# A merged attention, MLP and recurrence kernel: the gate reads the normalised output from PSUM, and TensorE takes two steps of its loop in another order

## The reference, cut to what matters

```python
# layer 0, last part
ln_out = layernorm(x, ln3_s, ln3_b)
x = x + gelu(ln_out @ w1 + b1) @ w2 + b2
# layer 1
xa = ln(x) * ln1_w + ln1_b
sx = previous token's xa - xa
xxx = tanh((xa + sx * maa_x) @ maa_w1)          # the mixer
xk, xw, xv, xr, xg = xa + sx * (maa_stack + xxx @ maa_w2)
w = exp(-exp(time_decay + tanh(xw @ td_w1) @ td_w2))
r, k, v = xr @ Wr.T, xk @ Wk.T, xv @ Wv.T
g = silu(xg @ Wg.T)
# per step and head: out = r . (u * k v + s);  s = k v + w * s
og = (out - mean_head) / sqrt(var_head + 1e-5)   # per head
og = og * gn_w + gn_b                            # the affine copy
x1 = x + (og * g) @ Wo.T                         # gate, output projection
# then the channel mix on x1: two shifts, key, receptance, value
```

## Time and profile before

| | |
|---|---|
| median of three runs | 1197.81 us (1195.29 to 1200.35) |
| span of the profiled execution, first to last instruction | 1193.3 us |
| its mean granted TensorE clock | 0.990 |
| PE busy | 1126.9 us (94%) |
| DVE busy | 968.7 us (81%) |
| ACT busy | 774.8 us (65%) |
| POOL busy | 594.3 us (50%) |
| the chain that ended last | PE 72%, DVE 16%, issue 8%, ACT 2% |

### The profile page before, as it was taken

How to read it: one execution, slowest core, us unless ns; L and a number is a source line. 1 busy time by engine, 2 the same in 40 slices (tenths; PEclk the granted TensorE clock), 3 DMA queues, 4 the chain that set the end, 5 groups by cost and what they waited for, 6 DMA issues and landing times.

```text
span 1193.3 us, 35515 instructions
## 1 busy us (share of the span) xinstructions
PE 1126.9 (94%) x13568; PEld 955.6 (80%) x13568; DVE 968.7 (81%) x1677; ACT 774.8 (65%) x1750; POOL 594.3 (50%) x520
## 2 busy tenths in 40 slices
PE   5899999999999999999999999999999999888898
PEld 5889898889989877777888788877888787667687
DVE  5987778787777761288999999999999999999964
ACT  5778777778778755556755566556755565557475
POOL 5787887877787840243343433434343434343221
PEclk9999999999999989999999999999999999989999
DMA  9400000011111100000000000000000000000001
GB/s 332 139 4 1 0 0 4 20 47 38 46 40 39 45 2 1 1 2 1 1 1 1 2 1 1 0 0 0 0 0 0 0 1 1 10 10 18 18 36 54
DMA packets 25535, 27.31 MB, mean 23 GB/s; under 512 B 2336, under 2 KB 20064, under 8 KB 25056
## 3 DMA queue, kind: packets, MB, share of 16 engines
q1 hardware_dynamic: 25440, 25.99, 6.6%
HBM read 21.79 MB, written 4.19 MB: 22 GB/s over the span
## 4 chain that ended last, share of the span: by engine, by line
PE 72%; DVE 16%; issue 8%; ACT 2%; POOL 1%; DMA 0%; DVEq 0%; ACTq 0%; POOLq 0%
PE psum L953 10%; PE psum L353 9%; PE psum L962 7%; PE psum L267 5%; PE psum L336 5%; PE psum L368 4%; PE psum L1042 4%; PE psum L297 3%; PE psum L1079 3%; DVE shared L1771 3%; PE psum L280 3%; DVE shared L1765 2%; PE psum L1127 2%; PE psum L310 2%; PE psum L1002 2%
## 5 line engine op out<-in xcount | busy, mean ns | idle before, releaser
L1771 DVE TENSOR_TENSOR_SCAN shared<-late_wT,shared 128x512 f32<-128x512 f32 x128 | 184.5, 1442 | 4.4
L863 POOL TENSOR_TENSOR late_xm<-late_mixed,late_xa 128x512 f32<-128x512 f32 x80 | 96.0, 1207 | 162.3 <-DVE late_mixed L1739 156.0
L232 POOL TENSOR_TENSOR shared<-shared,att_row_max 128x512 f32<-128x512 f32 x128 | 132.7, 1056 | 17.4 <-DVE att_row_max L564 17.4
L353 PE MATMUL psum<-shared 128*128 128x128 f32 x1024 | 126.2, 277 | 0.0
L453 ACT ACTIVATE shared<-shared 128x512 f32<-128x512 f32 x128 | 80.4, 631 | 67.9 <-POOL shared L232 67.8
L962 PE MATMUL psum<-w,late_hT 128*128 128x256 f32 x512 | 122.1, 383 | 1.0 <-ACT late_hT L1352 0.9
L872 POOL TENSOR_TENSOR shared<-shared,late_rT 128x512 f32<-128x512 f32 x32 | 41.1, 1284 | 163.6 <-DVE shared L1771 163.6
L353 PEld LDWEIGHTS psum<-shared 128*128 128x128 f32 x1024 | 120.6, 193 | 0.2 <-ACT shared L462 0.2
L564 DVE TENSOR_REDUCE att_row_max<-shared 128x8 f32<-128x512 f32 x128 | 86.9, 680 | 41.0 <-POOL shared L225 41.0
L953 PE MATMUL psum<-late_glnT,w 128*128 128x256 f32 x512 | 118.4, 384 | 1.8 <-ACT late_glnT L1343 1.8
L1765 DVE TENSOR_TENSOR shared<-psum,shared 128x504 f32<-128x504 f32 x128 | 86.7, 678 | 39.1 <-PE psum L1079 37.8
(11 more groups left out here) (170 smaller groups left out, 2656.7 us busy)
## 6 DMA issues: line engine op xcount, KB each, us to landing
shared<-in_enc SPq DMA_DIRECT2D x64, 128.0 KB, 2.6
out<-x SPq DMA_DIRECT2D x16, 256.0 KB, 2.0
x<-in_x SPq DMA_DIRECT2D x7, 512.0 KB, 9.0
w<-in_w SPq DMA_DIRECT2D x2, 1024.0 KB, 16.9
shared<-in_cross_mask SPq DMA_DIRECT2D x1, 1024.0 KB, 11.6
shared<-in_w_qkv SPq DMA_DIRECT2D x1, 768.0 KB, 4.5
x<-in_x SPq DMA_DIRECT2D x2, 256.0 KB, 3.7
shared<-in_w_kv SPq DMA_DIRECT2D x1, 512.0 KB, 12.6
```

Of the source, the lines that this page charges most:

```text
L232: nc.gpsimd.tensor_tensor(zs, zs, peak.unsqueeze(2).to_broadcast([P, PAIRS, S]), ALU.subtract).then_inc(shifted, 1)
L353: last = nc.tensor.matmul(dst[:, half * P:(half + 1) * P], w[:, kb, c0 + half * P:c0 + (half + 1) * P], src[:, u % 2, kb, 0:P], start=(kb ...
L863: nc.gpsimd.tensor_tensor(xm[:, m % 2, :, :].rearrange("p h (b t) -> p (h b) t", t=S), mixed[:, m % 2, :, :].rearrange("p h (b t) -> p (h ...
L1771: nc.vector.tensor_tensor_scan(states, wT[:, u, half, :, :, :].rearrange("p j b t -> p (j b t)"), states, 0.0, ALU.mult, ALU.add).then_inc ...
```

## The change

The affine copy writes its result back into its own PSUM bank (`even`) instead of the SBUF tile `onT`, and the gate reads it there. So the bank is busy for longer, and what next writes it (`bonus_sums`, and in the last run `transpose_on`) waits for `y_ready` instead of `onT_copied`. The copy itself no longer waits for the gate of the run before. On TensorE `bonus_sums(s)` and `project_out(s - 2)` move behind `mlp_transpose(s + 3)` and `mixer(s + 1)`.

```diff
-        onT = core.shared[:, 13328:13840]
@@ bonus_sums
                 if later(r - 1):
-                    pe.wait_ge(onT_copied, r - 1)
+                    pe.wait_ge(y_ready, r - 1)
@@ transpose_on
                 if is_last(r):
-                    pe.wait_ge(onT_copied, r)
+                    pe.wait_ge(y_ready, r)
@@ body of TensorE
                     if n == 1:
+                        if mlp_run:
+                            mlp_transpose(s + 3)
+                        if mixing:
+                            mixer(s + 1)
                         if now:
                             bonus_sums(s)
                         if there(s - 2):
                             project_out(s - 2)
-                        if mlp_run:
-                            mlp_transpose(s + 3)
-                        if mixing:
-                            mixer(s + 1)
@@ copy_on of ScalarE
-                if later(r):
-                    act.wait_ge(y_ready, r)
                 for half in range(HALVES):
-                    last = nc.scalar.activation(onT[...], even[...],
+                    last = nc.scalar.activation(even[...], even[...],
@@ apply_gate of VectorE
-                nc.vector.scalar_tensor_tensor(out=yT[:, :], in0=onT[:, :], scalar=0.5, ...
+                nc.vector.scalar_tensor_tensor(out=yT[:, :], in0=even, scalar=0.5, ...
```

More of the change, by code:

```diff
@@ L1456, in copy_on @@
                 act.wait_ge(onT_ready, r + 1)
-                if later(r):
-                    act.wait_ge(y_ready, r)
                 for half in range(HALVES):
-                    last = nc.scalar.activation(onT[:, half * RT:(half + 1) * RT], even[:, half * RT:(half + 1) * RT],
+                    last = nc.scalar.activation(even[:, half * RT:(half + 1) * RT], even[:, half * RT:(half + 1) * RT],
                                                 ACT.Identity, scale=col(core, "gn_w", half), bias=col(core, "gn_b", half))
@@ L1827, in apply_gate @@
                     dve.wait_ge(out_ready, r)
-                nc.vector.scalar_tensor_tensor(out=yT[:, :], in0=onT[:, :], scalar=0.5, in1=gates[:, u, :], op0=ALU.mult,
+                nc.vector.scalar_tensor_tensor(out=yT[:, :], in0=even, scalar=0.5, in1=gates[:, u, :], op0=ALU.mult,
                                                op1=ALU.mult).then_inc(y_ready, 1)
```

## The result

The changed kernel took 1234.82 us (median of four runs, 1233.11 to 1237.93) against 1198.79 us before: ratio 1.0316, 95% interval 1.029 to 1.0342. It is slower, as forecast, by 36 us where 25.7 were forecast. (The ratio is as recorded; the two medians alone give 1.030, inside the interval.) The median lies at the upper end of the forecast range of 1211 to 1235, and the ratio taken on the 1197.81 us of the forecast gives 1235.7, just beyond it. The span of the profiled execution went from 1193.3 to 1232.3 us, the mean granted clock from 0.990 to 0.985.

A forecast was written before the change was run, and what follows sets the result against it. The prediction took TensorE to bound the loop, 37.57 us of work in a 38.40 us period. Terms 18.7 + 2.15 + 1.6 + 2.3 + 1.0 = 25.7 us on 1197.8 gave 1223.5 us, range 1211 to 1235.

The forecast's parts named there:

- The transposes and the mixer wait for steps that stand behind the gate on DVE: On PE after spread(s, 1): both wait for DVE's residual and mixer input; +1.87 us in each of ten bodies.
- The gate 0.68 us, the fight with POOL handed on to the read, 0.60 us gained: DVE's gate L1828 falls from 1.51 to 0.68 us, POOL's L846 blocks the read L1782; DVE gains 0.60 us per body.
- The copy unchanged: ScalarE's affine copy pair, now writing PSUM, still takes 1.02 us, with 0.3 us either way.
- PE idles 2.2 us ... after another 0.35 us: PE, body 7: 2.2 us idle before the MLP's transposes L938, then 0.35 us more before the mixer.
- From the mixer's start to `spread(s, 2)`: PE, body 7: 2.49 us as after a gap, plus 2.64 us for bonus sums and projection with no wait.
- The clock: Rival: PE's gaps drop the clock to 1.2 GHz in four or more of 13 bodies, 2.3 us each, 1233 to 1253; chance 0.11.
- Body 13, 2.3 us: Body without MLP: 2.64 us put behind the mixer, DVE having perhaps 0.3 us slack; 2.3 us more, bounds 0 and 2.64.
- body 14, 1.0: Body 14 loses between 0 and 1.87 us, 1.0 taken.
- Bodies 0 and 1, 1.6: Bodies without a gate: bonus sums lose the wait that hides them, 0.81 us each, 1.6 us in all.
- Not slower: Rival: transposes and mixer fill the gate's wait and the shorter gate pulls everything forward, 1189 us, or near 1198; chance 0.08.
- half absorbed: Rival: DVE's slack shortens its later steps and PE's waits in bodies 12 to 15, 1204 to 1212 us; chance 0.04.
- gate still held up: Rival: PSUM as input brings nothing, DVE's chain stays, +2.47 us per body instead of 1.87, 1229.5 us; chance 0.05.

The follow-up runs named there:

- the order alone: Kernel before with only TensorE's changed order, the affine copy staying in SBUF: 1261.98 us, ratio 1.0535.
- DVE's order turned round: Changed kernel with mlp_residual and mixer_input put ahead of apply_gate and read in DVE's step 0: 1214.84 us, ratio 1.0137.
- the PSUM half alone: Changed kernel with TensorE's order of before, affine copy and gate still in PSUM: 1199.04 us, ratio 1.0017.
- the sums behind the mixer: Changed kernel with the two sum_heads directly behind mixer(s + 1), bonus sums and projection behind them: 1232.24 us, a single run.
- The filled gap: Changed kernel with the four transposes of spread(s, 1) done five times over in bodies 2 to 13: 1226.95 us, ratio 1.0243.
- the head sums in the gap: Changed kernel with the two sum_heads of run s - 1 moved ahead of mlp_transpose: 1214.70 us, ratio 1.0139.

## Why the prediction was right and wrong, point by point

The direction and the mechanism of the waits were right. Two steps of the sum failed. The larger is the clock: the sum has nothing for it, and it cost 9.2 us of the span. The smaller is the stretch from the mixer's start to `spread(s, 2)`, put at 5.13 us and measured at 5.44, 3.3 us over eleven bodies.

- *The transposes and the mixer wait for steps that stand behind the gate on DVE.* Right, shown by three runs: the order alone loses more, DVE's order turned round gives 1.0 us per period back, and the PSUM half alone does next to nothing.
- *The gate 0.68 us, the fight with POOL handed on to the read, 0.60 us gained.* Right: 0.66, 0.92, 0.61. The Trainium skill, page "SBUF — State Buffer", section "Who interferes with whom", says that a DVE instruction with at most one SBUF input, outside the 2-port modes, does not contend with GpSimd, and that one with two does when GpSimd reads SBUF. The trace agrees: beside POOL's operation the gate takes 0.66 us and the read 0.92.
- *The copy unchanged.* Right: 0.99 against 1.02 us. The page "ScalarE: Activation LUTs", section "Step-by-step: what each stage is for", of the Trainium skill says that ScalarE writes PSUM faster than SBUF. The trace agrees, by 0.03 us for the pair, too little to count.
- *"PE idles 2.2 us ... after another 0.35 us", mixer at 5.88 us after `transpose_on`.* Right: the mixer starts 5.87 us after it, in body 8.
- *"From the mixer's start to `spread(s, 2)`" 2.49 + 2.64 = 5.13.* This step failed by 0.3 us in each body: the measured 5.44. I took mixer and sums as one block of 2.49 us, but the change puts bonus sums and projection between them, and the two no longer overlap: 0.13 us. The bonus sums take 0.92 us to the next start and not 0.81, the projection 1.90 and not 1.83 (840.76, 841.68, 843.58): 0.18 more. With the sums behind the mixer the period is 40.33, which is near my 38.44 + 1.87 in part by luck: the stretch is 5.21 there, not 5.13, and the spread behind it is 0.05 shorter. The step is 3.3 us of the 13.3 by which the span's growth was missed.
- *The clock.* This is the larger error, 9 us. I made it a rival with a chance of 0.11, on the ground that the gap is framed by dense work, and left it out of the sum. The filled gap shows that the ground does not hold. A fall of the clock in the loop was one of my own signs of being wrong. My evidence was misread too: I wrote that longer gaps in the tail had no such sequel, but behind the waits of 2.27 and 1.41 us in body 13 of the kernel before (they end at 1021.59 and 1024.99), this window shows one:

```profile
1027.00:1030.00 3.00, 3.00 (x20) 0.50 0.00 0
```

  The price per fall was wrong as well: 1.3 us in the short ones and 3.2 to 3.3 in the long ones, not 2.3. Four falls came behind the new gaps, in bodies 2, 7, 11 and 13, at 9.2 us together. The rival had put 1233 us on four of them, and the kernel took 1234.8; that these are so near is in part luck, since two falls cost 1.3 us and two 3.2 to 3.3, where four at 2.3 were assumed, and the 3.3 us of the step above are not in the 1233.
- *Body 13, 2.3 us.* Right without the clock fall behind the mixer's wait, as the filled gap shows; *body 14, 1.0*: 0.6. *Bodies 0 and 1, 1.6*: 2.0; what the 0.4 are stays open.
- *Not slower, half absorbed, gate still held up.* None of them: nothing was given back in bodies 2 to 12.

What decides in which bodies the clock falls was not separated from the gap's place in time. That it is not the gap's length alone, the traces show in body -1, where all ten kernels run the same code and the mixer waits some 2.18 us, until between 480.5 and 484.5 us. Within 1.6 us of the wait's end the clock falls in four of them: the PSUM half alone, DVE's steps forward, and the head sums in either place. The window in the kernel before, and the same in the kernel with the PSUM half alone (us, busy and count, granted clock):

```profile
482.00:485.00 3.00, 2.34 (x15) 1.00 0.00 0
```

```profile
482.00:485.00 3.00, 3.00 (x11) 0.50 0.00 0
```

## What to carry to other kernels

A step is moved ahead of a wait only if its own inputs are ready by then: read when the other engine produces them, in that engine's own order. Here 0.8 us of waiting became 2.6 (2.20 from the end of the spread, 0.44 us after its start at 835.71, to 838.35, and 0.36 ahead of the mixer). The best filler is work whose inputs are a whole stage old, here the head sums, and what its old neighbours lose by its leaving is part of the price. When an edit opens a gap of about 2 us on TensorE, add to the sum, for each gap, a chance times the price of running the next microseconds at 1.2 GHz. Here that price was 1.3 to 3.3 us.

## What the runs showed of the hardware

- Gaps and clock in bodies 2 to 12, one trace of each kernel: waits of up to 1.16 us (the kernel before, the PSUM half alone, DVE's steps forward, the head sums in the gap) had no fall in 44 bodies, though body 1 of the PSUM half alone had one behind its wait of 1.21 us; waits of 2.03 to 2.16 us, with a second of some 0.3 behind, had 3 of 11 and 5 of 11; 2.63 to 2.73 us had 8 of 11, and there they repeat in every body from 6 to 12. The same wait of 2.18 us in body -1 had 4 in ten traces.
- Transposes in the gap kept the clock at 2.4 GHz: 16 more of them per body cost no time and saved some 8 us by the medians.
- Two float32 matmul groups with 32 output rows overlapped when adjacent: 2.49 us for mixer and sums against 2.62 apart, and a group's length depended by 0.05 to 0.1 us on its neighbour.
